# Expert products of a group made in one row in the exponential buffers, with Gelu reading them there

## What is computed

```python
s, i = top_k(sim, 8)                  # 8 heads, two halves of 32 keys each
all_scores = sx[..., :, None] + sy[..., None, :]
scores, pk = top_k(all_scores, 8)     # the best 8 of the pairs of a head
o = einsum('bnd,bnhkd->bnhk', inputs, key_in[idx])
o = gelu(o, approximate=False) * softmax(scores)
out = einsum('bnhk,bnhkd->bnd', o, key_out[idx])
```

## Time and profile before

| | |
|---|---|
| median of 3 runs | 1721.02 us (1718.32 to 1722.32) |
| the profiled execution, its own time | 1717.66 us |
| its span | 1715.9 us |
| busy, share of the span | DVE 88%, PE 87%, POOL 78%, ACT 74% |
| attention, then feed-forward | to about 715 us, from there to the end |

### The profile page before, as it was taken

One profiled execution on the slowest core, in us unless ns is written; L12 is line 12 of the kernel. 1 busy time (PEld: TensorE's weight loads), 2 busy tenths in 40 slices (PEclk: granted clock), 3 DMA queues, 4 the chain that ended last, 5 costly groups with the idle time before them and its releaser, 6 DMA issues.

```text
span 1715.9 us, 33034 instructions
## 1 busy us (share of the span) xinstructions
PE 1490.5 (87%) x10688; PEld 1029.4 (60%) x10688; DVE 1502.3 (88%) x4488; ACT 1264.6 (74%) x1741; POOL 1330.6 (78%) x1579
## 2 busy tenths in 40 slices
PE   3799999999999998678888888888888888888877
PEld 2355555555555554367667666676666766667766
DVE  3889999999999985389999999999999999999998
ACT  1166666666666666378888888888888888888885
POOL 1055555556655556499999999999999999999993
PEclk9799999999999999789999999999999999999999
DMA  5344445444555440100000000000000000000000
GB/s 139 88 99 105 109 111 118 111 110 103 119 113 111 103 103 22 62 1 19 1 20 20 1 19 19 7 13 19 19 1 20 20 1 19 19 8 13 14 7 7
DMA packets 73627, 86.37 MB, mean 50 GB/s; under 512 B 9872, under 2 KB 63760, under 8 KB 68752
## 3 DMA queue, kind: packets, MB, share of 16 engines
q1 hardware_dynamic: 73456, 84.27, 20.7%
HBM read 58.30 MB, written 25.95 MB: 49 GB/s over the span
## 4 chain that ended last, share of the span: by engine, by line
POOL 47%; issue 5%; ACT 3%; DVE 2%; PE 1%; ACTq 0%; DVEq 0%; SPq 0%
POOL SUM L772 47%; ACT E L873 2%; DVE W L965 2%; ACT L807 1%; ACT GE L806 0%; PE WT L1033 0%; PE MB L1000 0%; PE E L988 0%; DVE CT L948 0%; DVE M8Y L909 0%; DVE SMALL L926 0%; ACT L806 0%; ACT SIM L800 0%; PE MB L975 0%; DVE SMALL L909 0%
## 5 line engine op out<-in xcount | busy, mean ns | idle before, releaser
L772 POOL TENSOR_TENSOR SUM<-SIM 128x1024 f32<-128x1024 f32 x512 | 958.5, 1928 | 11.5 <-DVE W L965 7.9
L965 DVE SCALAR_TENSOR_TENSOR W<-SUM,SMALL,E 128x1024 f32<-128x1024 f32 x512 | 641.9, 1279 | 46.4 <-ACT E L873 44.7
L873 ACT ACTIVATE E<-SUM,NB 128x1024 f32<-128x1024 f32 x512 | 566.6, 1118 | 102.1 <-DVE W L965 86.9
L1033 PEld LDWEIGHTS WT<-idf,W 128*128 128x128 f32 x4096 | 497.3, 151 | 231.3 <-DVE W L965 120.6
L1033 PE MATMUL WT<-idf,W 128*128 128x128 f32 x4096 | 570.8, 292 | 69.3 <-DVE CT L948 38.0
L261 POOL TENSOR_SCALAR_AFFINE_SELECT PT<-PT 128x128 f32<-128x128 f32 (+1 forms) x1024 | 336.9, 355 | 257.8 <-ACT PT L355 224.2
L414 DVE CUSTOM_DVE_ANT_0 SY<-SY,bandf 128x384 f32<-128x384 f32 x512 | 273.3, 574 | 0.0
L355 ACT ACTIVATE PT<-TX 128x512 f32<-128x512 f32 x256 | 153.0, 598 | 113.6 <-PE TX L542 113.4
L429 DVE TENSOR_REDUCE mx<-SX 128x2 f32<-128x512 f32 x256 | 174.5, 682 | 59.8 <-PE SX L524 59.7
L357 ACT ACTIVATE PT<-TY 128x768 f32<-128x768 f32 x256 | 207.4, 810 | 3.7
L570 PE MATMUL PV<-PT,V 128*32 128x384 f32 (+1 forms) x2048 | 165.5, 441 | 2.6 <-POOL PT L261 2.4
(11 more groups left out here) (110 smaller groups left out, 1638.9 us busy)
## 6 DMA issues: line engine op xcount, KB each, us to landing
K<-k_parts SPq DMA_DIRECT2D x96, 192.0 KB
Q<-q_parts SPq DMA_DIRECT2D x288, 64.0 KB
q_parts<-qp SPq DMA_DIRECT2D x16, 384.0 KB, 2.4
k_parts<-kp SPq DMA_DIRECT2D x16, 384.0 KB, 2.4
xin<-in_x SPq DMA_DIRECT2D x16, 256.0 KB, 3.1
xres<-in_x SPq DMA_DIRECT2D x16, 256.0 KB, 9.5
x<-X SPq DMA_DIRECT2D x16, 256.0 KB, 2.2
x2T<-X2T SPq DMA_DIRECT2D x16, 256.0 KB, 2.1
```

Source lines behind the costliest of these rows:

```text
L772: return eng.tensor_tensor(SUM[(q * FH + h) % RING][:, :].rearrange("p (i j) -> p i j", i=NK), sx, sy, ALU.add)
L873: nc.scalar.activation(E[h % 2][:, :], SUM[(k * FH + h) % RING][:, :], ACT.Exp, bias=NB[q][:, h:h + 1]).then_inc(S["exp_ready"], 1)
L965: nc.vector.scalar_tensor_tensor(out=W[h % WRING][:, :], in0=SUM[(k * FH + h) % RING][:, :], scalar=TOP[q][:, h, TOPK - 1:TOPK], in1=E[h % ...
L1033: o = pe.matmul(WT[:, e, :], W[h % WRING][:, e * P:(e + 1) * P], ident[:, :], is_transpose=True, start=(h == 0 and e % 4 == 0), stop=(h == ...
```

## The change

In the third tile of each group (`k == BURST`, 2) PE makes all eight products of the next group at `h == 0`, ahead of that head's transposes. They go into the four halves of `E[1]` and `E[0]`, and from the fifth on each waits for the Gelu that has read its half. ACT, at `h == 1` and ahead of that head's exponential, loads the Gelu table, applies Gelu to each product out of `E` straight into `GE`, and loads the other table again. The copies through `MB`, the Gelus over 2048 columns and the semaphore between them go. DVE does, at `h == 1` of that tile and behind `experts`, parts 0 to 5 of the search for the next tile and parts 0 to 4 for the one behind it; the first two tiles of a group do parts 0 to 5 in pairs at `h` = 2, 3 and 4, and the last tile has part 5 alone at `h == 4`.

```diff
-EVEN_PARTS = ((), (), (), (), ((1, 0), (1, 1), (1, 2), (1, 3), (1, 4), (1, 5), (2, 0), (2, 1)), (), ((1, 6),), ((1, 7),))
-ODD_PARTS = ((), (), ((1, 2),), ((1, 3),), ((1, 4), (1, 5)), (), ((1, 6),), ((1, 7),))
+BURST = 2
+NORMAL_PARTS = ((), (), ((1, 0), (1, 1)), ((1, 2), (1, 3)), ((1, 4), (1, 5)), (), ((1, 6),), ((1, 7),))
+BURST_PARTS = ((), ((1, 0), (1, 1), (1, 2), (1, 3), (1, 4), (1, 5), (2, 0), (2, 1), (2, 2), (2, 3), (2, 4)), (), (), (), (), ((1, 6),), ((1, 7),))
+LATER_PARTS = ((), (), (), (), ((1, 5),), (), ((1, 6),), ((1, 7),))
+PARTS = (NORMAL_PARTS, NORMAL_PARTS, BURST_PARTS, LATER_PARTS)
...
+    def expert_bank(j, e):
+        return E[(j * FH + 1 + e // 2) % 2][:, e % 2 * GN:(e % 2 + 1) * GN]
...
-        def gelus(g, b, half):
-            act.wait_ge(S["expert_copied"], g * BLK + (half + 1) * 4)
-            o = GE[b][:, 4 * half:4 * half + 4, :].rearrange("p e n -> p (e n)")
-            nc.scalar.activation(o, o, ACT.Gelu).then_inc(S["gelu_ready"], 1)
+        def experts_gelu(j, g, b):
+            wait_pos(act, S["experts_weighted"], (g - 1) * GT)
+            nc.scalar.preload_act_table_set("gelu_and_others")
+            for e in range(BLK):
+                act.wait_ge(S["expert_product"], g * BLK + e + 1)
+                nc.scalar.activation(GE[b][:, e, :], expert_bank(j, e), ACT.Gelu).then_inc(S["expert_copied"], 1)
             nc.scalar.preload_act_table_set("natural_log_exp_and_others")
-        def o_copy(g, b, e):
-            act.wait_ge(S["expert_product"], g * BLK + e + 1)
-            nc.scalar.copy(GE[b][:, e, :], MB[:, :]).then_inc(S["expert_copied"], 1)
+            act.wait_ge(S["expert_copied"], (g + 1) * BLK)
...
+                    if h == 1 and k == BURST and more:
+                        experts_gelu(j, g + 1, 1 - b)
...
+                    if h == 1 and real:
+                        experts(*prev)
+                    for ahead, part in PARTS[k][h]:
                         if more or k < GT - ahead:
                             choose(part, j + ahead, (k + ahead) % 4, (k + ahead) % 2)
-                    if h == 1 and real:
-                        experts(*prev)
...
-        def o_block(b, e):
-            pe.matmul(MB[:, :], key_in[:, e * P:(e + 1) * P], X2T[b][:, :], start=True, stop=True).then_inc(S["expert_product"], 1)
+        def experts_in(j, g, b):
+            for e in range(BLK):
+                if e == 0:
+                    pe.wait_ge(S["x2T_loaded"], (g + 1) * 16)
+                    pe.wait_ge(S["weights_masked"], j * FH)
+                if e == 2:
+                    pe.wait_ge(S["weights_masked"], j * FH + 1)
+                if e >= 4:
+                    pe.wait_ge(S["expert_copied"], g * BLK + e - 3)
+                pe.matmul(expert_bank(j, e), key_in[:, e * P:(e + 1) * P], X2T[b][:, :], start=True, stop=True).then_inc(S["expert_product"], 1)
...
-                    if h == SLOT_A and more:
-                        pe.wait_ge(S["x2T_loaded"], (g + 2) * 16)
-                        pe.wait_ge(S["sim_copied"], j + 3)
-                        pe.wait_ge(S["expert_copied"], (g + 1) * BLK + 2 * k)
-                        o_block(1 - b, 2 * k)
+                    if h == 0 and k == BURST and more:
+                        experts_in(j, g + 1, 1 - b)
...
-                    if h == SLOT_B and more:
-                        pe.wait_ge(S["sim_copied"], j + 4)
-                        o_block(1 - b, 2 * k + 1)
```

More of the change, by code:

```diff
@@ L665 @@
 WRING = 8
-EVEN_PARTS = ((), (), (), (), ((1, 0), (1, 1), (1, 2), (1, 3), (1, 4), (1, 5), (2, 0), (2, 1)), (), ((1, 6),), ((1, 7),))
-ODD_PARTS = ((), (), ((1, 2),), ((1, 3),), ((1, 4), (1, 5)), (), ((1, 6),), ((1, 7),))
+BURST = 2
[3 more added lines that the diff above has]
+PARTS = (NORMAL_PARTS, NORMAL_PARTS, BURST_PARTS, LATER_PARTS)
 SIM0 = 2
-SLOT_A, SLOT_OUT, SLOT_SIM, SLOT_B = 0, 2, 4, 6
-COPY_B, COPY_A, COPY_OUT, COPY_SIM = 1, 3, 5, 7
+SLOT_OUT, SLOT_SIM = 2, 4
+COPY_OUT, COPY_SIM = 5, 7
 def ffn(nc, ctx, x1, x2T, KM, key_in, key_out, gb, ident, bnst, first, out):
@@ L719, in ffn @@
              "sim_product sim_copied pair_sums exp_ready weights_masked weights_turned "
-             "experts_weighted out_product out_copied expert_product expert_copied gelu_ready "
+             "experts_weighted out_product out_copied expert_product expert_copied "
              "out_stored ranked candidates top_ready top_less_max top_exp exp_sum log_sum bias_ready").split()
@@ L828, in _ @@
             nc.scalar.activation(GE[0][:, e, :], E[e // 2 % 2][:, e % 2 * GN:(e % 2 + 1) * GN], ACT.Gelu).then_inc(S["expert_copied"], 1)
-        act.wait_ge(S["expert_copied"], BLK)
-        act.sem_inc(S["gelu_ready"], 2)
         nc.scalar.preload_act_table_set("natural_log_exp_and_others")
@@ L878, in group @@
                         small_ln(j + 1)
[L879 to L882, removed]
         steps(act, group)
@@ L945, in experts @@
             dve.wait_ge(S["weights_turned"], (j + 1) * FH)
-            dve.wait_ge(S["gelu_ready"], (g + 1) * 2)
+            dve.wait_ge(S["expert_copied"], (g + 1) * BLK)
             wait_pos(dve, S["out_product"], j - 1)
@@ L956, in group @@
                 for h in range(FH):
-                    for ahead, part in (ODD_PARTS if k % 2 else EVEN_PARTS)[h]:
+                    if h == 1 and real:
+                        experts(*prev)
+                    for ahead, part in PARTS[k][h]:
                         if more or k < GT - ahead:
                             choose(part, j + ahead, (k + ahead) % 4, (k + ahead) % 2)
-                    if h == 1 and real:
-                        experts(*prev)
                     dve.wait_ge(S["exp_ready"], j * FH + h + 1)
@@ L1007, in group @@
                 for h in range(FH):
-                    if h == SLOT_A and more:
-                        pe.wait_ge(S["x2T_loaded"], (g + 2) * 16)
-                        pe.wait_ge(S["sim_copied"], j + 3)
-                        pe.wait_ge(S["expert_copied"], (g + 1) * BLK + 2 * k)
-                        o_block(1 - b, 2 * k)
+                    if h == 0 and k == BURST and more:
+                        experts_in(j, g + 1, 1 - b)
                     if h == SLOT_OUT and real:
                         pe.wait_ge(S["sim_copied"], j + 3 if more or k < 2 else GROUPS * GT)
-                        pe.wait_ge(S["expert_copied"], (g + 1) * BLK + (2 * k + 1 if more else 0))
                         wait_pos(pe, S["out_copied"], j - 1)
```

## The result

The changed kernel takes 1772.22 us in the median (1770.79 to 1776.11, 4 runs), the kernel before 1719.67 us on the same chip (1713.83 to 1722.32, 4 runs): a ratio of 1.0314, 95% interval 1.0281 to 1.0347. The forecast was 1774 us in a range of 1747 to 1790.

A forecast was written before the change was run, and what follows sets the result against it. The prediction took the exponential-and-mask loop between ACT and DVE as the bound, with POOL 1.5 us a group faster. Per group -2.4 + 3.4 + 2.4 + 0.25 = +3.65 us, 15 bursts 54.8, about +1 more: 1774 us, range 1747 to 1790.

The forecast's parts named there:

- what the change takes away: DVE's waits for late transposes, the even tile's Gelu and a copy vanish: 1.20 us in two tiles, 2.4 a group.
- DVE's wait ahead of `m1`: Third tile, mask of `h == 1`: DVE ready at 9.10, mask starts about 12.5 behind PE-paced Gelus, so 3.4 us waiting.
- `m5` late, at full clock: Third tile, mask of `h == 5`: four masks take 5.79 us instead of 4.80 behind queued outputs and copy, 1.0 us late.
- the clock on top of it: PE behind its 3.7 us idle time in the third tile: the clock falls, costing nothing to 1.75 us; 1.4 taken.
- last tile of the group, with the split of the searches: Last tile: ACT's copy shows through with only part 5 between masks, 0.25 us; splitting searches in the first two tiles costs nothing.
- The 0.60 us of `CT`: DVE's `CT` starts 3.07 us behind a pair of masks instead of 2.47, for late transposes; this loss was to go.
- the 0.48 of the Gelu: Even tile: DVE waits 0.48 us before the next mask for the 2048-column Gelu with two table loads; to go.
- the 0.12 of the copy: Copy at `h == 3`: three masks take 3.72 us to the next start instead of 3.60; the 0.12 was to go.
- the shape of this stall: Run's last tile: masks in a row, ACT's copy waiting 0.78 us for PE, four masks taking 5.79 us instead of 4.80.
- the 1.75 that was called the most: Upper limit of the clock's cost behind the burst: eight transposes 0.8 us slower and `outputs` some 0.95 more.
- the fall behind 2.30 us: Earlier trace: after 2.30 us idle, PE's 16 transposes took 3.40 us instead of 2.19; counted as agreeing with the skill's rule.
- The bound of a gain: Whole feed-forward loop: a gain is at most 1.5 us a group, 22 us, since then POOL becomes the bound.

The follow-up runs named there:

- e4: Changed kernel without the loop's expert products and Gelus, every group reading the first group's values, all tiles searching like an ordinary one: 1690.76 us, ratio 0.9848.
- e3: Changed kernel with each product made for only 256 of its 512 columns, so half the expert values are wrong: 1735.07 us, ratio 1.0107.
- e1: Changed kernel plus four unread products in PE's idle time in the third tile: 1756.58 us, ratio 1.0229 to the kernel before.
- e7: e2 plus products made earlier, more search in the gap, and the first product put into `MB`: 1717.89 us, ratio 0.9998 to the kernel before.
- e2: Changed kernel with PE making the third tile's `outputs` at `h == 1`, ahead of its idle time: 1748.25 us, ratio 1.0193 to the kernel before.
- e10: Changed kernel plus unread products only, four in the third tile and one in the last tile of each group: 1744.47 us, ratio 1.0157.
- e8: e2 plus one unread product in PE's idle time in the last tile of each group: 1735.45 us, ratio 1.0103 to the kernel before.
- e9: e7 plus one unread product in PE's idle time in the last tile of each group: 1709.35 us, ratio 0.9953 to the kernel before.

## Why the prediction was right

Its steps, for one group of the profiled execution:

| term | predicted | measured |
|---|---|---|
| what the change takes away | -2.4 | -2.9 (4 x 14.64 = 58.56 from 61.46) |
| DVE's wait ahead of `m1` | 3.4 | 3.21 to 3.46 printed, `m1` at 12.40 (12.5) |
| `m5` late, at full clock | 1.0 | 1.00 (5.80 - 4.80), in two bursts |
| the clock on top of it | 1.4 | 1.30 to 2.55 in 13 of 15 bursts, 1.45 in the mean of all |
| last tile of the group, with the split of the searches | 0.25 | about 0.4, what remains of 21.38 + 12.63 - 2 x 14.64 = 4.73 |
| falls in the last tile | none | 1.37 in 3 of 15 groups, 0.27 in the mean |
| sum | +3.65 | +3.49 |

**The waits that go.** The 0.60 us of `CT`, the 0.48 of the Gelu and the 0.12 of the copy all went: in the changed kernel `CT` waits for PE nowhere. The term was mis-sized by 0.5 us, as e4 shows too, where a group takes 58.56 before POOL bounds it. Between the rows shown in the earlier trace rows, the candidates start 0.86 us behind the searches that they read (1413.61 to 1414.47), a batch that is not read at once only 0.76 ahead of what follows; with the searches split by masks that 0.10 goes too, once in two tiles, 0.2 in a group. Another 0.1 is that the two tiles of the earlier trace rows give 61.36 for a group, and the mean is 61.46. I did not follow up the rest.

**The burst.** This step held throughout: the rows of the first group's products gave the pace of 0.86 us, and e3 shows that it is PE's. The Trainium skill, page "ScalarE: Activation LUTs", section "Table sets: the hidden batching unit", asks for calls batched by table set; they are batched here, and a table load still takes 1.28 us. Only the 0.48 us in two tiles named above is won: the group's four loads stood mostly in ACT's waiting before (an argument from the earlier trace rows, not tried by itself), and of the two that remain the second now stands ahead of a mask that DVE waits for.

**Behind the burst.** That the last tile of the run shows the shape of this stall at full clock was right to 0.01 us, and e1 makes all 15 bursts behave so. PE's idle time of 3.7 us was 3.57. The fall of the clock was taken at less than its whole. Where it came it mostly cost 1.63, nearly the 1.75 that was called the most, and once 2.55; in two bursts it cost nothing. The Trainium skill, page "TensorE: Matmul & The Clock Gate", section "Why this matters for your kernels", would have the fall in every burst; the trace agrees in 13 of 15, and in the two others the same 3.57 us passed without it. The prediction also counted the fall behind 2.30 us as agreeing with that section; its advice is on longer gaps, so that row goes beyond it.

**What the prediction left out.** Falls in the last tile of a group. It read from the earlier trace rows that the clock stays full behind 1.41 us of idle time, and took that for a property of 1.41 us. It held in the last group, and in three of 15 others it did not. In this kernel that costs 4 us; in e7, where all else is better, it is nine groups and takes back nearly the whole gain.

**The bound of a gain.** "At most 1.5 us a group ... 22 us" was too small: e4 is 26 us under the kernel before. This touched no chance.

That the number came out within 2 us of the measured time is in part luck. The clock, taken too small where it fell and too large where it held, came to 21.7 / 15 = 1.45 us in the mean, close to the 1.4. The other errors cancel: 0.5 us too little taken away, against 0.15 in the last tile and 0.27 for the falls there. And the last step was not carried out: a median 3.4 us above a profiled execution of 1773 makes 1776 to 1777, not the 1774 to which it was rounded.

What stays open: which condition decides whether and when the clock falls behind the same idle time, and whether useful work could replace the unread products. Neither was tried, nor was moving the `sim_copy` at `h == 7`, which keeps its 0.5 us in each tile.

## What to carry to other kernels

A burst that fills a gap of one engine must be counted on every engine that feeds it: here ACT's and DVE's gap was ready, but PE hands over a product every 0.86 us, and the 8 x 0.86 stood on the path. Then look at what stands in line behind the engine that waits: an output, its copy and the next exponential were all queued behind PE's idle time, and moving the output ahead of it (e2) took nearly the whole second stall away. Where a matmul engine idles just ahead of work on the path, a product that nobody reads can be cheaper than the slow clock behind the gap; try it as an experiment even if it doesn't stay, since it prices the clock by itself.

## What the runs showed of the hardware

- The same idle time of PE, 1.41 us in the last tile of a group, was followed by a full clock in some groups and by the lower one in others of the same execution: falls in 3 of 15 groups in the changed kernel, 5 in e1, 9 in e7, none in the profiled e2. So an idle time seen once with the clock at 1.00 proves nothing of the next one of the same length.
- The clock fell eight times in the first two tiles of a group in e10, and no tile took longer for it.
- Behind an idle time of 3.56 us the clock was still 1.00 for 0.94 us of matmuls in one burst and fell then; in later bursts, with the same idle time and work, it fell some 0.07 us earlier from burst to burst (changed kernel).
- In the profiled executions, one unread product of 128x512 in that idle time removed all falls there (e8, e9, e10); four in the 3.57 us of the third tile removed all falls there (e1, e10).
- Gelus of 512 columns last 0.60 us each, but start 0.478 apart when nothing holds them up (e3).
